# Expert blocks of 128 rows in place of 256, in a mixture-of-experts layer with a recurrent branch

## Time and profile before

| | |
|---|---|
| time, median of 3 runs | 570.37 us (569.82 to 572.63) |
| profiled execution, span from first to last instruction | 547.8 us |
| its own time | not listed apart from the span; the median is 22.6 us above the span |
| TensorE busy | 466.4 us, 85%, 3896 matmuls |
| weight loads | 377.0 us, 69%, 3897 |
| VectorE busy | 326.6 us, 60% |
| ScalarE busy | 224.5 us, 41% |
| GpSimd busy | 273.9 us, 50% |
| mean granted TensorE clock | 0.945 |
| expert stage | 150.6 to 486.2 us of the span |

### The profile page before, as it was taken

How to read it: one execution, slowest core, us unless ns; L and a number is a source line. 1 busy time by engine, 2 the same in 40 slices (tenths; PEclk the granted TensorE clock), 3 DMA queues, 4 the chain that set the end, 5 groups by cost and what they waited for, 6 DMA issues and landing times.

```text
span 547.8 us, 13251 instructions
## 1 busy us (share of the span) xinstructions
PE 466.4 (85%) x3896; PEld 377.0 (69%) x3897; DVE 326.6 (60%) x583; ACT 224.5 (41%) x354; POOL 273.9 (50%) x547
## 2 busy tenths in 40 slices
PE   1866668679689899999999999999999999999521
PEld 1753345344468788888888888888888888866321
DVE  4998896578635444554544545545445455448976
ACT  4963337455753333333332433423324333316450
POOL 4617887878722434344343443443444434445784
PEclk9999797799889999999999999999999999999756
DMA  8803659565440324312122121121221211019644
GB/s 261 276 4 108 221 175 313 218 228 176 150 143 20 106 83 153 96 45 68 52 73 58 58 66 58 56 68 48 76 58 56 74 57 39 20 44 370 242 153 153
DMA packets 42051, 64.69 MB, mean 118 GB/s; under 512 B 5037, under 2 KB 30768, under 8 KB 42032
## 3 DMA queue, kind: packets, MB, share of 16 engines
q1 hardware_dynamic: 33408, 46.34, 26.9%
q0 software_dynamic: 6816, 16.92, 8.7%
q10 hardware_dynamic: 1808, 1.19, 0.7%
HBM read 40.93 MB, written 25.33 MB: 121 GB/s over the span
## 4 chain that ended last, share of the span: by engine, by line
issue 32%; POOL 23%; PE 17%; DMA 16%; DVE 7%; POOLq 2%; ACT 2%; DVEq 0%; SPq 0%; ACTq 0%
DMA y_dram<-rows_raw 13%; POOL slots_dram L403 9%; PE bankC L944 5%; PE bankB L944 5%; PE bankA L944 4%; POOL stat L372 2%; POOL y_dram L449 2%; DMA w_raw<-x_in 2%; DVE w_raw L841 1%; POOL rows_raw L436 1%; POOL rows_raw L440 1%; POOL spare L432 1%; PE bankD L1012 1%; POOL rows_raw L428 1%; POOL spare L447 1%
## 5 line engine op out<-in xcount | busy, mean ns | idle before, releaser
L944 PE MATMUL bankA<-rows_raw,w_raw 128*128 128x256 f16 x936 | 110.2, 275 | 2.0 <-DVE rows_raw L854 2.0
L944 PE MATMUL bankC<-w_raw,rows_raw 128*128 x936 | 109.2, 273 | 0.4 <-DVE rows_raw L862 0.3
L944 PE MATMUL bankB<-rows_raw,w_raw 128*128 128x256 f16 x936 | 108.6, 273 | 0.0
L944 PEld LDWEIGHTS bankA<-rows_raw,w_raw 128*128 x936 | 92.0, 99 | 14.1 <-issue 2.7
L944 PEld LDWEIGHTS bankC<-w_raw,rows_raw 128*128 128x128 f16 x936 | 90.0, 98 | 14.3 <-issue 2.6
L944 PEld LDWEIGHTS bankB<-rows_raw,w_raw 128*128 x936 | 91.5, 98 | 10.3
L449 POOL DMA_INDIRECT y_dram<-rows_raw x78 | 79.2, 1015 | 32.8 <-issue 32.8
L403 POOL DMA_INDIRECT slots_dram<-rows_raw,pos_i x64 | 74.0, 1156 | 30.9 <-issue 20.1
L862 DVE TENSOR_TENSOR rows_raw<-rows_raw 128x512 f16<-128x512 f32 x78 | 54.0, 693 | 55.7 <-ACT rows_raw L622 55.7
L859 DVE SCALAR_TENSOR_TENSOR rows_raw<-rows_raw,bankA 128x512 f32<-128x512 f32 x39 | 26.8, 687 | 92.9 <-ACT rows_raw L617 92.9
L617 ACT ACTIVATE rows_raw<-bankA 128x512 f32<-128x512 f32 x39 | 23.3, 597 | 128.5 <-PE bankA L944 128.5
(11 more groups left out here) (151 smaller groups left out, 670.4 us busy)
## 6 DMA issues: line engine op xcount, KB each, us to landing
work<-w_exp_in SPq DMA_DIRECT2D x24, 512.0 KB, 5.2
rows_raw<-slots_dram SPq DMA_DIRECT2D x39, 260.0 KB
w_raw<-y_dram SPq DMA_DIRECT2D x8, 1024.0 KB, 14.1
w_raw<-x_in SPq DMA_DIRECT2D x9, 512.0 KB, 4.2
out<-w_raw SPq DMA_DIRECT2D x8, 512.0 KB, 2.9
work<-x_in SPq DMA_DIRECT2D x7, 512.0 KB, 4.6
slots_dram<-fill SPq DMA_DIRECT2D x9, 260.0 KB, 4.9
y_dram<-rows_raw POOLq DMA_INDIRECT x78, 2.4
```

The costliest lines, as they stand in the source:

```text
L944: last = pe.matmul(out_ap, lhsT, rhs, start=(n == 0), stop=(n == len(todo) - 1))
```

## The change

`BLOCK` becomes 128 and `BLOCKS` 71. A block's inner layer is one tensor of two banks: bank 0 has the four outputs of a, bank 1 those of b, 128 columns each; blocks alternate between bankA and bankB. PE computes all of a (24 matmuls of 128 columns), transposes the next block, then computes all of b (24), then the last block's outputs (12 of 256 columns, into half of a bank). ACT and DVE have one silu, one product, one high part and one low part per block, of 128 x 512. Loaded rows and outgoing rows get four buffers (`DEEP`), and SP loads and GpSimd prepares gates for two blocks at once. PE's and DVE's loops run over four blocks. The block tables grow with `BLOCKS` and three small ones share a tensor.

```diff
-BLOCK = 256
-SB = BLOCK // P
+BLOCK = P
+DEEP = 4
+PAIRS = BLOCKS // 2
...
+            def load_pair(b, half, n_blocks=2):
+                if not isinstance(b, int) or b >= DEEP:
+                    sp.wait_ge(slot_t_ps, b - 2)
+                    sp.wait_ge(meta_ready, b - 2)
+                for j in range(n_blocks):
+                    load_slots(b + j, 2 * half + j)
...
+            def scatter_pair(q, half, again=True, next_blocks=2):
+                scatter_y(q, 0, half)
+                meta(q + 1, 1 - half, again, next_blocks)
+                scatter_y(q, 1, half)
...
+            def hidden_act(b, i, before, last=False):
+                act.wait_ge(h_ps, b * 2 + 1)
+                if before >= 2:
+                    act.wait_ge(g_ready, b - 1)
+                act.activation(sil[i], AB[i][:, 0, :].rearrange("p (m n) -> p m n", m=KH), ACT.Silu,
+                               scale=1.0 / WSCALE).then_inc(sil_ready, 1)
+                if not last:
+                    high_slots(b + 1, 1 - i, before == 0)
+                act.wait_ge(g_ready, b + 1)
+                if before >= 2:
+                    act.wait_ge(y_ps, b - 1)
+                act.activation(g_hi[i], g32[i], ACT.Copy).then_inc(g_hi_ready, 1)
...
+            def one_block(b, i, before=None, last=False):
                 if not last:
                     low_slots(b + 1, 1 - i)
-                half(b, i, 1)
+                product(b, i)
+                if before is not None:
+                    gate_y(*before)
+                product_low(b, i)
...
-            def hidden(b, i, j, off, first):
-                if not first:
-                    pe.wait_ge(g_ready, b * 2 - 1 + j)
-                for m in (2 * j, 2 * j + 1):
-                    for half in range(2):
-                        col = half * HID + m * P
-                        last = three(AB[j][:, m % 2, half * BLOCK:half * BLOCK + BLOCK], range(KD),
+            def hidden(i, half, off):
+                for m in range(KH):
+                    col = half * HID + m * P
+                    last = three(AB[i][:, half, m * BLOCK:m * BLOCK + BLOCK], range(KD),
...
-                for s in range(SB):
-                    last = three(bankC[:, i, s * D:s * D + D], range(KH),
+                three(bankC[:, i, 0:D], range(KH),
...
                 off = weights_at(b)
                 pe.wait_ge(slot_lo_ready, b + 1)
-                hidden(b, i, 0, off, first)
+                if not first and not second:
+                    pe.wait_ge(g_ready, b - 1)
+                hidden(i, 0, off)
                 if first:
                     pe.wait_ge(z_ready, EARLY)
                 if not last:
-                    transpose_slots(b + 1, 1 - i, first)
-                hidden(b, i, 1, off, first)
+                    transpose_slots(b + 1, j, loaded, first)
+                hidden(i, 1, off)
...
+            with pe.Fori(DEEP + 2, BLOCKS - 4, DEEP) as b:
+                for n in range(DEEP):
+                    j = (DEEP + 2 + n + 1) % DEEP
+                    one_block(b + n, n % 2, j, b * 4 + (4 * (n + 1) - 4 * j + 16))
```

More of the change, by code:

```diff
@@ new lines, in _ @@
+            load_pair(0, 0)
+            load_pair(2, 1)
+            for b in range(4, 2 * X_EARLY + 4, 2):
+                load_pair(b, b // 2 % 2)
+                c = b // 2 - 2
+                if c == 0:
+                    sp.wait_ge(w_lo_ready, EARLY * PIECES)
+                    sp.wait_ge(p_lo_ready, KD * (EARLY - 1))
+                tiles = slice(c * TPC, (c + 1) * TPC)
+                sp.dma_start(x_early[:, tiles, :], x_v[:, tiles, :]).then_inc(x_early_loaded, 16)
+            with sp.Fori(2 * X_EARLY + 4, BLOCKS - 4, 4) as b:
+                load_pair(b, 1)
+                load_pair(b + 2, 0)
@@ new lines, in scatter_y @@
+            def scatter_y(q, j, half):
+                pool.wait_ge(y_sb, q * 2 + j + 1)
+                pool.wait_ge(meta_ready, q * 2 + 2)
+                pool.tensor_tensor(spare[:, 2 + j:3 + j], spare[:, 6:7], spare[:, 6:7], ALU.add)
+                i = 2 * half + j
+                pool.indirect_dma_start(
+                    out=y_dram, out_offset=bass.IndirectOffsetOnAxis(dest[half][:, j:j + 1], 0),
+                    in_=ys[:, i, :], in_offset=None,
+                    bounds_check=ROWS_OUT - 1, oob_is_err=False).then_inc(y_scattered[i], 16)
@@ L608, in high_slots @@
                 act.activation(xT[i][:, 0:KD, :], slots_ps_of(b, i), ACT.Copy).then_inc(slot_hi_ready, 1)
[L610 to L616, removed]
-                    act.activation(sil[j], AB[j][:, :, 0:BLOCK], ACT.Silu,
-                                   scale=1.0 / WSCALE).then_inc(sil_ready, 1)
-                    act.wait_ge(g_ready, b * 2 + j + 1)
-                    if before >= 2:
-                        act.wait_ge(y_ps, b - 1)
-                    act.activation(g_hi[i][:, 2 * j:2 * j + 2, :], g32[j], ACT.Copy)\
-                       .then_inc(g_hi_ready, 1)
+            def hidden_act(b, i, before, last=False):
[10 more added lines that the diff above has]
+                act.activation(g_hi[i], g32[i], ACT.Copy).then_inc(g_hi_ready, 1)
             repeat(act, 1, EARLY - 1, 1, recur)
@@ L866, in gate_y @@
+            def gate_y(b, q, j, first):
                 dve.wait_ge(y_ps, b + 1)
-                dve.wait_ge(meta_ready, b + 1)
+                dve.wait_ge(meta_ready, q * 2 + 2)
                 if not first:
-                    dve.wait_ge(y_scattered[i], b * 16 if i == 0 else b * 16 - 16)
-                for s in range(SB):
-                    last = dve.scalar_tensor_tensor(ys[i][:, s, :], bankC[:, i, s * D:s * D + D],
-                                                    gate_c[i][:, s:s + 1], half_bias,
-                                                    ALU.mult, ALU.add)
@@ L875, in gate_y @@
-                last.then_inc(y_sb, 1)
-            def halves(b, i, last=False):
-                half(b, i, 0)
+                    dve.wait_ge(y_scattered[j], b * 4 - 4 * j)
+                half = j // 2
+                dve.scalar_tensor_tensor(ys[:, j, :], bankC[:, b % 2 if isinstance(b, int) else j % 2, 0:D],
+                                         gate_c[half][:, j % 2:j % 2 + 1], half_bias,
+                                         ALU.mult, ALU.add).then_inc(y_sb, 1)
+            def one_block(b, i, before=None, last=False):
@@ L893, in _ @@
-            halves(BLOCKS - 1, 0, True)
-            gate_y(BLOCKS - 2, 1, False)
-            gate_y(BLOCKS - 1, 0, False)
+            for b in range(1, DEEP + 1):
+                one_block(b, b % 2, (b - 1, (b - 1) // 2, b - 1, True))
+            one_block(DEEP + 1, 1, (DEEP, DEEP // 2, 0, False))
+            with dve.Fori(DEEP // 2 + 1, PAIRS - 1, 2) as q:
+                for j in range(DEEP):
+                    one_block(q * 2 + j, j % 2, (q * 2 + (j - 1), q + (j - 1) // 2, (j + 1) % DEEP, False))
@@ L898, in sum_y @@
+            one_block(BLOCKS - 1, 0, (BLOCKS - 2, PAIRS - 1, (BLOCKS - 2) % DEEP, False), last=True)
+            gate_y(BLOCKS - 1, PAIRS, (BLOCKS - 1) % DEEP, False)
             def sum_y(c):
```

217 lines of the change are left out of this document (94 added, 123 removed).

## The result

The changed kernel takes 739.84 us (median of 4 runs, 738.42 to 743.45) against 570.5 us (median of 4, 569.82 to 572.63): ratio 1.298, 95% interval 1.294 to 1.303, so about 30% slower. Predicted were 762 us (722 to 800). The profiled execution took 738.8 us, of which its span is 737.0.

The account below looks back on a forecast made before the run. The sequencer feeding TensorE was taken to bound the expert stage at 7.4 us a block: stage +191.3 us and block list 0.5 bring the span from 547.8 to 739.6, plus 22.6 around it, 762 us (722 to 800).

Parts of the forecast that it names:

- The sequencer sets the pace once matmuls have 128 columns: Expert stage: TensorE's instruction sequencer, at 7.4 us a block against the array's 4.3, limits the changed kernel; chance 0.80.
- The signs named for it: Expert-stage trace: 16 + 16 + 8 addresses at 0.127 us, "issue" idling, weight loads far below today's share, clock 1.00.
- 40 addresses at 0.128 us, 5.1 us a block: PE's queue, each 128-row block: 32 inner-layer and 8 output address instructions, as many as before, 5.1 us.
- Two reads of 0.9 us: PE's queue, each block: weight-offset reads for this block and the last one, 0.8 and 1.1 us, together 1.8 us.
- 7.4 us a block, from the two-block count of the kernel before: Sequencer's time per new block: 7.6 us measured before, less 0.13 for loop ends and up to 0.1 for fewer matmuls.
- The count from parts: Sequencer's time per new block: addresses 5.1, reads 1.8, loop end 0.1, transposes and their waits 0.3, together 7.3 us.
- The array needs 4.3 us a block: Matrix array, each new block: 48 inner matmuls, 12 output matmuls and 2 transposes take 4.1 to 4.4 us, 4.3 taken.
- Case A: Expert stage: matmuls pass at the array's rate whatever the address instructions take, stage 307 us, time 544 us; chance 0.08.
- Case B: Expert stage: weight loads of 98 ns stop overlapping short matmuls, 6.2 us a block, time 679 us; chance 0.04.
- Case C: Expert stage: TensorE's clock falls to half, 8.3 us a block, time 828 us; chance 0.05.
- The start doesn't move: Start of the expert stage: the first block's matmuls begin at 152.9 us, before and after the change.
- 22.6 us around the span: Outside the profiled span: the median of 570.37 us stands 22.6 us above 547.8, added unchanged to the predicted span.

Follow-up runs that it names:

- Experiment 1: The changed kernel with weights always at expert 0's fixed address, so no offset reads or address instructions in the expert stage: 533.46 us, ratio 0.936.
- Experiment 3: The changed kernel with the last block's weight offset kept in its register, dropping the second read for 54 of 71 output layers: 701.66 us, ratio 1.231.
- Experiment 4: The kernel before with 24 instead of 16 address instructions per inner half and one more offset read a block: 632.18 us, ratio 1.109.
- Experiment 5: The changed kernel with only the b half of the inner layer at expert 0's fixed address, both reads kept: 642.04 us, ratio 1.125.
- the last experiment: GpSimd's first scatters wait for routing, fourteen up front: kernel before, also with kept offset register in second blocks, 561.95 us; changed kernel, wait alone, 730.37 us.

## Why the prediction was right, and where its numbers weren't

- *The sequencer sets the pace once matmuls have 128 columns.* Right. Experiments 1, 3, 4 and 5 move the stage by the sequencer's work alone, in both directions and on both kernels. The signs named for it came: 16 + 16 + 8 addresses, stops by "issue", clock 1.00 from 175 us on. Only the weight loads fell less far than "far below their share" says, from 289.59 of 335.6 us to 191.20 of 295.
- *40 addresses at 0.128 us, 5.1 us a block.* Right: 16, 16 and 8, 0.127 apart.
- *Two reads of 0.9 us.* The starts in the sequencer's rows give 0.7 and 0.9, and a read taken away gives 0.67 back. With 5.1 to 5.3 for addresses, 1.6 for reads, 0.1 for the transposes (predicted 0.3) and 0.1 for the loop's end this is 6.9 to 7.1; measured 7.12.
- *7.4 us a block, from the two-block count of the kernel before.* This is the term that was mis-sized: 7.12, inside the bounds of 6.9 to 7.8, so the stage grew by 172.6 us and not 191.3. The count from parts had said 7.3, and the count from the period was the worse of the two. It had put 0.2 us a block back for handing over, without a row for it; without that it gives 7.2. Whether the rest is time in which the old loop's sequencer waited for the array isn't shown.
- *The array needs 4.3 us a block*. 4.21 measured. The Trainium skill's 81 ns a matmul at 128 columns (TensorE: Matmul & The Clock Gate, "Back-to-back issue gap") stands against 56 ns in experiment 1's stream of loads and matmuls at clock 1.00, and the measurement decides. The changed kernel does show 86 ns, but that is 16 addresses in 24 matmuls, and goes with them.
- *Case A, 544 us, array-bound.* Its price was nearly that of experiment 1 (533.46 us); its condition failed, for 7.0 us of sequencer stand against 4.2 of array.
- *Case B, loads that don't overlap, 679 us.* Experiment 1 rules it out: 24 loads and matmuls in 1.34 us.
- *Case C, the clock falls.* No: 0.66 from 170 to 175 us, after TensorE had stood for 3.10 us, and 1.00 from there to 676 us, with TensorE idle for 17% of the time.
- *The start doesn't move.* As between the two kernels, right (163.01 and 162.45 in the last experiment); as read from the one profile, 17.2 us off, since that execution lacked the standstill and its last scatter came 16.2 us earlier.
- *22.6 us around the span.* Wrong. The time of an execution is 1.8 us above its span (738.8 and 737.0). It is 1.8 in every other run, too, and the kernel before's timed executions have spans of 563.7 to 571.4 us. So the 22.6 were mostly that its profiled execution, with a span of 547.8, was some 20 us faster than its timed ones. The two errors have this one cause and opposite signs: +17.2 in the span, -20.8 around it. That the predicted span, 739.6, lies so near the measured 737.0 is luck: the stage was 18.7 us shorter and began 17.2 us later.
- Sum of the deviations: -18.7 for the stage's length, +17.2 for its start, -20.8 around the span, -1.1 for the tail and block list, +1.0 between the profiled execution and the median: -22.4, where 739.84 - 762 is -22.2.

## What to carry to other kernels

Before a tile is halved, ask which instructions halve with it. Address arithmetic and reads of run-time values are per operand slice, not per column: they stayed at 40 and 2 a block, and were paid 71 times in place of 39. The busy shares didn't show that limit here. Look at the starts of the sequencer's rows, and compare their sum with the array's time for the smallest tile planned. And when the median stands 20 us above a profiled span, look for a second profile before calling the difference overhead.

## What the runs showed of the hardware

- Matmuls of 128 columns in fp16, each with its own 128 x 128 weight load from a fixed address, started 0.056 us apart in a stream at clock 1.00 (experiment 1).
- A run-time address took 0.127 us of the sequencer at clock 0.50 and at 1.00, with the array full or standing, and a read of a value 0.67 us. Pairs of load and 8-column matmul without one started 0.026 us apart; that handing such pairs over is hidden behind addresses, and not when these go, is inferred from experiment 5.
- A burst of GpSimd's indirect transfers went with 18.8 us of standstill on DVE and slowed issue on TensorE in the changed kernel, and with neither in the one profile of the kernel before; the cause is open. To hold the burst back until the routing was done brought 9.5 us on the changed kernel, and 7.9 us (with one read less in each second block) on the kernel before.
